# Row-tiled maxima in runs of two pairs, with K, V and Q in the output bank of V

## The chip, the cores and the metric

One core of a Trainium2 chip runs one program. The metric is its device time in microseconds. A time difference of less than half a per cent is not told from none here.

## What is computed

`x` is 2048 tokens by 128. The layer is a LayerNorm, attention with 16 heads of 64, and a mixture of 8 experts of which each token takes one, all added to `x`:

```python
xn = _layernorm(x)
q, k, v = (xn @ Wq), (xn @ Wk), (xn @ Wv)           # each cut into 16 heads of 64
attn = softmax(q @ k.T * 64 ** -0.5)                # per head, 2048 x 2048
attention = (attn @ v) @ Wo + bo
expert_ids = argmax(softmax(xn @ router_w.T))
h = square(relu(xn @ expert_fc[e]))                 # 128 -> 512
ffn = h @ expert_proj[e].T                          # 512 -> 128, of each token's own expert
return x + attention + ffn
```

## The kernel before, in words

Heads go in pairs (8 pairs), and a pair's queries in 4 chunks of 512: 32 blocks, written out one after another. Block n handles two heads and 512 queries. The instructions of each engine are one hand-written order; engines meet at semaphores.

A block has 16 steps `kt`, one for each tile of 128 keys. In a step, TensorE (PE) computes the scores of both heads, transposed: keys on partitions, queries along 512 columns. Each score is two matmuls into one of three banks `SB` (`high_scores`, `low_scores`), since Q and K are split into a high and a low part of fp32r: `K1` holds K's high part twice, `Q1` Q's high part in the 64 rows of the head's own half and the low part in the other half; `K2` and `Q2` carry K's low part, a row of ones and a row of minus the maximum. So the maximum is already subtracted when the bank is full. ACT takes the exponential of each bank (`exps`) into `EX`. After step 15 PE multiplies V by the exponentials (`times_v`), both heads in 64 columns each side by side in the bank `OB`, fp32, and ACT copies `OB` to `osb` (`take_o`). POOL adds the exponentials of one head, and of the other up to step 8 or 9; DVE adds the rest behind the scores. `fold_sums` (a transpose and a reduce of 512 columns) and `sum_parts` (five small steps) make the reciprocal row; SyncE stores it and spreads it to 128 partitions, POOL scales (`normalise`), and PE multiplies by Wo (`project`).

The maxima that block n+1 needs are made in block n, one matmul of [128 x 128] x [128 x 512] for each of 32 units (2 heads, 4 query tiles, 4 key chunks), one behind each score tile, into a ring of three banks `MB` (`max_unit`); DVE reduces each bank to one column (`maxima`). Block 0's own maxima are made ahead of it from 64 rows of each head, two heads as a pair (`max_pair`), with one reduce of 1024 columns for both (`maxima_pair`).

The eighth bank `XB` takes what comes in between: Q of block n+2 (step 14), V of the pair (steps 1, 2, 6, 8 of its first block), K of the next pair (steps 2 and 7 of its second and third block), the experts' products (steps 4 and 11), and Wo. `take_spare` makes each user of the bank wait until the one before has been read.

ACT copies a K or Q product into `high`, DVE makes `low` from the product minus `high`, and SyncE issues six DMAs that put the two into `K1`, `K2` or `Q1`, `Q2`. `high` may be written again only when those have landed: this is `staging_free`, a wait of ACT. For Q in a block that also makes K, it waits for both K chunks of that block. `K1` and `K2` have one semaphore for each parity of the pair (`d_k`).

SyncE's queue is in one order for each block, `one(n)` in its part: first K chunk (`spread_k`), row store and spread (`store_row`, `spread_rd`), the tokens of the next tile (`load_tokens`, four DMAs), second K chunk, Wo's weights, the expert's result (`store_tile`), the expert's weights (`load_tile`: a register is read from `owner_i`, then two DMAs), the maxima row (`place_max`), Q (`spread_q`). The tokens are sorted by expert into 23 tiles of 128; a tile goes with each of the blocks 5 to 27. POOL's indirect DMAs sort the tokens in blocks 1 to 3 (`SORT`) and fetch the results in blocks 28 to 30.

In the blocks of `LATE` the sums of the second head are folded in step 1 of the next block, in the others behind the scores.

## Time and profile before

| | |
|---|---|
| median of 3 runs | 1355.83 us (1352.04 to 1357.24) |
| profiled execution | 1357.17 us, its span 1355.4 us |
| PE busy | 1333.3 us, 98% |
| DVE busy | 1199.6 us, 89% |
| POOL busy | 1121.8 us, 83% |
| ACT busy | 708.4 us, 52% |
| mean granted clock of TensorE | 0.988 |

The span is from the first instruction to the last on the core. A matmul's record is longer than its distance to the next, since matmuls are pipelined: what one costs is seen from one start to the next. A block of the middle takes 39.6 us, 41.0 us when it makes K, and 43.2 us when it makes V. The clock is at half for the first 53 us but for one short stretch, and then at full.

### The profile page before, as it was taken

Reading aid. Unit: us, or ns where it says so; the run is one execution under the profiler, and the core shown is the slowest. Engines: PE = TensorE matmul, PEld = TensorE weight load, DVE = VectorE, ACT = ScalarE, POOL = GpSimd, SP = SyncE. Lnnn points to the kernel's source line nnn. Section 1 sums busy time; section 2 is a strip of 40 time slices with the busy share of each in tenths; the row PEclk is TensorE's granted clock in tenths of the full one; section 3 lists DMA queues with packets and bytes.
Section 4 is the critical chain, followed back from the end, with each engine's and each line's share of the span. In section 5 each row is a group of like instructions: output and inputs, shape, how many; then the busy total and the mean of one; then the engine's idle time right before and its main releaser. Section 6 shows DMA issues by size and latency. Waiting matters only on the chain.

```text
span 1355.4 us, 20239 instructions
## 1 busy us (share of the span) xinstructions
PE 1333.3 (98%) x6268; PEld 865.0 (64%) x6268; DVE 1199.6 (89%) x1890; ACT 708.4 (52%) x1230; POOL 1121.8 (83%) x884
## 2 busy tenths in 40 slices
PE   6999999999999999999999999999999999999998
PEld 3656667666676666776666766666766667765554
DVE  7788998998988899889988899889898899989997
ACT  4454556444565444664445664445654446654453
POOL 6779989787987778977788877879878789888997
PEclk8799999999999999999999999999999999999999
DMA  4223311233203222124212241124311143011101
GB/s 117 77 55 83 100 31 41 68 85 75 52 28 86 71 71 51 51 64 100 50 43 57 72 103 34 42 57 100 75 47 38 41 101 94 14 37 34 41 17 40
DMA packets 85867, 82.76 MB, mean 61 GB/s; under 512 B 24512, under 2 KB 54912, under 8 KB 85760
## 3 DMA queue, kind: packets, MB, share of 16 engines
q1 hardware_dynamic: 84736, 79.38, 23.5%
q0 software_dynamic: 1024, 2.10, 0.5%
q8 instruction: 50, 0.82, 0.3%
q14 instruction: 57, 0.47, 0.1%
HBM read 27.00 MB, written 6.29 MB: 25 GB/s over the span
## 4 chain that ended last, share of the span: by engine, by line
PE 93%; DVE 4%; ACT 1%; issue 1%; DMA 0%; POOL 0%; DVEq 0%; POOLq 0%
PE OB L1182 33%; PE SB L1127 16%; PE SB L1134 16%; PE MB L1153 15%; PE XB L1220 3%; PE XB L1210 2%; PE XB L1115 2%; PE XB L1108 2%; DVE low L935 2%; ACT high L677 1%; DVE mx L785 1%; PE XB L1191 1%; PE XB L1189 1%; PE XB L1190 1%; PE OB L1090 1%
## 5 line engine op out<-in xcount | busy, mean ns | idle before, releaser
L539 POOL TENSOR_TENSOR acc<-acc,ex 128x512 f32<-128x512 f32 x691 | 912.1, 1345 | 29.5 <-ACT ex L663 1.6
L785 DVE TENSOR_REDUCE mx<-MB 128x1 f32<-128x512 f32 x992 | 652.0, 684 | 72.5 <-PE MB L1153 71.5
L663 ACT ACTIVATE ex<-SB 128x512 f32<-128x512 f32 x1024 | 608.5, 599 | 103.9 <-PE SB L1134 40.2
L1182 PE MATMUL OB<-ex,V 128*64 128x512 f32 x2048 | 447.2, 594 | 0.0
L1127 PE MATMUL SB<-Q,K 128*128 128x512 f32 x1024 | 411.6, 402 | 0.0
L1134 PE MATMUL SB<-Q,K 128*128 128x512 f32 x1024 | 400.2, 391 | 0.0
L1153 PE MATMUL MB<-K,Q 128*128 128x512 f32 x992 | 389.5, 393 | 1.5 <-DVE mx L785 1.5
L1182 PEld LDWEIGHTS OB<-ex,V 128*64 128x64 f32 x2048 | 143.9, 137 | 277.8 <-issue 274.2
L821 DVE TENSOR_TENSOR acc<-acc,ex 128x512 f32<-128x512 f32 x205 | 285.2, 1391 | 20.1 <-DVE acc L821 0.9
L693 ACT ACTIVATE osb<-OB 128x512 f32<-128x512 f32 x32 | 19.2, 599 | 458.4 <-PE OB L1182 458.4
L1127 PEld LDWEIGHTS SB<-Q,K 128*128 128x128 f32 x1024 | 192.9, 188 | 66.4 <-issue 27.6
L539 POOL TENSOR_TENSOR acc<-ex 128x512 f32<-128x512 f32 x63 | 79.9, 1290 | 177.3 <-ACT ex L663 169.5
L1153 PEld LDWEIGHTS MB<-K,Q 128*128 128x128 f32 x992 | 186.4, 188 | 51.4 <-DVE mx L785 11.3
L1134 PEld LDWEIGHTS SB<-Q,K 128*128 128x128 f32 x1024 | 193.1, 189 | 35.7
L950 DVE STREAM_TRANSPOSE rd<-acc 128x512 f32<-128x512 f32 x62 | 44.0, 710 | 4.7 <-POOL acc L539 1.1
L952 DVE TENSOR_REDUCE halves<-rd 128x16 f32<-128x512 f32 x62 | 42.5, 686 | 2.2
L544 POOL TENSOR_TENSOR osb<-osb,rd 128x512 f32<-128x512 f32 x31 | 40.4, 1304 | 2.6 <-DMA rd<-rows_rd 2.6
L1220 PEld LDWEIGHTS XB<-wo,osb 128*128 128x128 f32 x248 | 30.2, 191 | 14.0 <-DVE low L935 13.8
L935 DVE SCALAR_TENSOR_TENSOR low<-XB,high 128x512 fp32r<-128x512 f32 x31 | 21.4, 692 | 18.6 <-ACT high L677 18.6
L1220 PE MATMUL XB<-wo,osb 128*128 128x128 f32 x248 | 35.7, 287 | 1.6
L1210 PEld LDWEIGHTS XB<-wraw,xT 128*128 128x128 f32 x256 | 33.9, 193 | 2.7 <-ACT V L687 0.2
L1210 PE MATMUL XB<-wraw,xT 128*128 128x128 f32 x256 | 34.0, 276 | 0.0
(135 smaller groups left out, 630.0 us busy)
## 6 DMA issues: line engine op xcount, KB each, us to landing
Q<-high SPq DMA_DIRECT2D x124, 128.0 KB, 2.3
K<-high SPq DMA_DIRECT2D x112, 128.0 KB, 2.3
Q<-low SPq DMA_DIRECT2D x64, 128.0 KB, 2.3
rd<-rows_rd SPq DMA_DIRECT2D x62, 128.0 KB, 2.9
K<-low SPq DMA_DIRECT2D x56, 128.0 KB, 2.4
w<-fc SPq DMA_DIRECT2D x23, 256.0 KB, 2.8
w<-projT SPq DMA_DIRECT2D x23, 256.0 KB, 3.1
sorted_x<-res SPq DMA_DIRECT2D x1, 1472.0 KB, 6.8
```

The costliest lines, as they stand in the source:

```text
L539: pool.tensor_tensor(a[:, :], src[:, :], EX[h][kt][:, :], ALU.add).then_inc(done, 1)
L663: act.activation(EX[h][kt][:, :], SB[bank_of(n, 2 * kt + h)][:, :], ACT.Exp).then_inc(a_e[h], 1)
L785: dve.tensor_reduce(mx[:, m % 2, u:u + 1], MB[bank_of(m, i)][:, :], AX.X, ALU.max).then_inc(v_m, 1)
L821: dve.tensor_tensor(a[:, :], src[:, :], EX[0][kt][:, :], ALU.add).then_inc(sums[0][n % 2], 1)
L935: dve.scalar_tensor_tensor(out=low[:, :], in0=XB[:, :], scalar=SCALE, in1=high[:, :], op0=ALU.mult, op1=ALU.subtract).then_inc(v_q, 1)
L950: dve.transpose(turned[:, :], acc[h][n % 2][:, :]).then_inc(v_turn, 1)
L1127: pe.matmul(SB[bank_of(n, 2 * kt + h)][:, :], K1[par][h][:, keys], Q1[k][h][:, :], start=True, stop=False)
L1134: pe.matmul(SB[bank_of(n, 2 * kt + h)][:, :], K2[par][h][:, keys], Q2[k][h][:, :], start=False, stop=True).then_inc(t_s, 1)
L1153: pe.matmul(MB[bank_of(m, i)][:, :], Q1[k][h][:, q * P:(q + 1) * P], K1[par][h][:, c * QB:(c + 1) * QB], start=True, stop=True).then_inc(t ...
L1182: mm = pe.matmul(OB[own[h], :], V[:, k, own[h]], EX[h][k][:, :], start=(k == 0), stop=(k == NT - 1))
L1210: mm = pe.matmul(XB[:, k * P:(k + 1) * P], xT[:, tok], wraw[pair % 2][:, 2, :], start=True, stop=True)
L1220: mm = pe.matmul(XB[:, q * P:(q + 1) * P], on[:, q * P:(q + 1) * P], wo_s[pair % 2][:, :], start=True, stop=True)
```

## The change

All blocks now get their maxima from the 64 rows of each head's own half, that is from the high parts alone, two heads as a pair. The pairs come in runs of two, at the even steps (in block 0 at steps 4, 5, 7, 8, 10, 11, 13, 14), in four banks `MB`. `XB` is gone: it is the fourth bank of `MB`. K, V and Q products go through `OB`, V's output bank, K at steps 1 and 5, V at 1, 3, 5, 7, Q at 11. The first V moves in front of block 0, between its pairs. Wo and the experts' two products move to the end of the block, ahead of V's product, into the banks of `MB`; the first product of a tile is made one block ahead of the second. Four small steps of the sums (`sum_parts`) move behind the scores where the block is not in `LATE`; in `LATE`, now without block 3, they stand at steps 3, 5, 7, 9. In the queue of SyncE, the expert's weights are loaded ahead of the second K chunk, with a register read for each, and the result is stored last. The experts and the sorting start one block earlier.

```diff
@@ constants
-AT_Q, AT_WO, AT_ON = 14, 13, 6
-AT_V, AT_K, AT_LOW = (1, 2, 6, 8), (2, 7), 5
-AT_UP, AT_DOWN = 4, 11
+AT_Q, AT_WO = 11, 13
+AT_V, AT_K, AT_LOW = (1, 3, 5, 7), (1, 5), 9
 TILES = NT + E - 1
-TILE0 = 5
+TILE0 = 4
...
-LATE = (0, 1, 2, 3, NB - 4, NB - 3)
+LATE = (0, 1, 2, NB - 4, NB - 3)
@@ banks
-        MB_all, SB_all = bank("MB", 3), bank("SB", 3)
+        MB_all, SB_all = bank("MB", 4), bank("SB", 3)
...
-        OB, XB = bank("OB"), bank("XB")
+        OB, FB = bank("OB"), MB[3]
+        WO_B, DOWN_B, UP_B, WO_LAST, SUM_B = MB[0], MB[1], MB[2], MB[2], MB[3]
@@ where maxima stand
-        def units(n, kt, h):
...
+        def runs(n, kt):
+            places = (4, 5, 7, 8, 10, 11, 13, 14) if n.off == 0 else range(0, NT, 2)
+            if n.off == NB - 1 or kt not in places:
                 return []
...
+            i = places.index(kt)
+            return [2 * i, 2 * i + 1]
@@ kv_job
-            if j == 0 and kt in AT_V:
+            if j == 0 and n.off and kt in AT_V:
@@ ahead of block 0
-        BETWEEN = {0: ("t", 2), 2: ("t", 3), 5: ("k", 2), 6: ("q", 1), 7: ("r", 0), 8: ("k", 3), 9: ("r", 1), 10: ("r", 2),
-                   11: ("r", 3)}
+        BETWEEN = {0: ("t", 2), 2: ("t", 3), 4: ("k", 2), 5: ("v", 0), 6: ("k", 3), 7: ("q", 1), 8: ("r", 0), 9: ("v", 1),
+                   10: ("r", 1), 11: ("v", 2), 12: ("r", 2), 13: ("v", 3), 14: ("r", 3)}
@@ SyncE
-                def load_tile(r):
...
-                    e = sp.value_load(owner_i[0:1, bass.ds(r.place(1), 1)], min_val=0, max_val=E - 1)
...
+                def expert(r):
+                    return bass.ds(sp.value_load(owner_i[0:1, bass.ds(r.place(1), 1)], min_val=0, max_val=E - 1), 1)
+
+                def load_up(r):
+                    wait(sp, t_up, r.times(1))
+                    sp.dma_start(w1[:, :], fc[expert(r), :, :].rearrange("e d h -> d (e h)")).then_inc(d_up, 16)
+
+                def load_down(r):
+                    wait(sp, t_down, r.times(1))
+                    sp.dma_start(w2[:, :, :], projT[expert(r), :, :].rearrange("e (c p) d -> p (e c) d", p=P)).then_inc(d_down, 16)
...
-                    if has_tile(n + 1):
-                        load_tokens(n + 1 - TILE0)
+                    for r in tile_up(n + 1):
+                        load_tokens(r)
+                    for r in tile_up(n):
+                        load_up(r)
+                    for r in tile_down(n):
+                        load_down(r)
                     for job in kv_job(n, AT_K[1]):
                         if job[0] == "k":
                             spread_k(*job[1:])
...
-                    if has_tile(n):
-                        store_tile(n - TILE0)
-                    if n.off == TILE0 - 1:
-                        sp.wait_ge(v_own, 1)
-                    if has_tile(n + 1):
-                        load_tile(n + 1 - TILE0)
                     if n.off < NB - 1:
                         place_max(n + 1)
                     if n.off < NB - 2:
                         spread_q(n + 2)
+                    for r in tile_down(n):
+                        store_tile(r)
@@ POOL
-                        if kt == AT_ON and not (n.i is None and n.off == 0):
+                        if n.off and kt == (8 if n.off - 1 in LATE else 6):
                             normalise(n - 1)
@@ DVE
                     for kt in range(NT):
-                        for h in range(2):
-                            for m, u in units(n, kt, h):
-                                maxima(m, u)
+                        for p in runs(n, kt):
+                            maxima_pair(n + 1, p)
                         if 0 < n.off < NB - 1:
-                            late = n.off - 1 in LATE
-                            if late and kt == 1:
-                                fold_sums(n - 1, 1)
-                            sum_parts(n - 1, kt - late)
+                            if n.off - 1 in LATE:
+                                if kt == 1:
+                                    fold_sums(n - 1, 1)
+                                if kt % 2:
+                                    sum_parts(n - 1, kt // 2)
...
                         if n.off not in LATE:
                             fold_sums(n, 1)
-                        if n.off == NB - 2:
                             for part in range(1, 5):
                                 sum_parts(n, part)
@@ PE
-                def max_unit(m, i, u=None):
...
+                def max_pair(m, p):
...
+                        if p < 2:
+                            boundary_read(m - 2)
+                        wait(pe, v_m, m.times(UNITS, 2 * p - 2))
...
+                    for h in range(2):
+                        pe.matmul(PAIR[m.off > 0][p % 2][:, h * QB:(h + 1) * QB], Q1[k][h][own[h], q * P:(q + 1) * P],
+                                  K1[par][h][own[h], c * QB:(c + 1) * QB], start=True, stop=True).then_inc(t_m, 1)
...
                 def project(n):
-                    take_spare(v_y, n.times(1, 1))
+                    into = WO_B if n.off < NB - 2 else WO_LAST
+                    if n.off < NB - 2:
+                        wait(pe, v_m, (n + 3).times(UNITS, -2))
...
                             low_scores(n, kt, h)
-                            for m, u in units(n, kt, h):
-                                max_unit(m, u)
-                        if has_tile(n):
-                            if kt == AT_UP:
-                                expert_up(n - TILE0)
-                            if kt == AT_DOWN:
-                                expert_down(n - TILE0)
+                        for p in runs(n, kt):
+                            max_pair(n + 1, p)
...
                             project(n - 1)
+                        for r in tile_down(n):
+                            expert_down(r, n)
+                        for r in tile_up(n):
+                            expert_up(r, n)
                         times_v(n, 0, NT)
```

## Rows read from the trace of the kernel before

In a row of a timeline: start in us, duration in us, engine, line, operation, output<-inputs, count, and in brackets the idle time in front of it with what ended it. In a row of windows: the stretch, its length, busy time and count of PE, PEld, DVE, ACT and POOL, the granted share of TensorE's clock, the DMA share, GB/s.

**Rows 1.** The page, part 1: busy time and share of the span.

```profile
PE 1333.3 (98%) x6268; PEld 865.0 (64%) x6268; DVE 1199.6 (89%) x1890; ACT 708.4 (52%) x1230; POOL 1121.8 (83%) x884
```

**Rows 2.** The page, part 4: the chain that ended last.

```profile
PE 93%; DVE 4%; ACT 1%; issue 1%; DMA 0%; POOL 0%; DVEq 0%; POOLq 0%
```

**Rows 3.** Busy time by engine in block 5, V product to V product.

```profile
279.73:320.71 40.98, 40.92 (x195) 26.89 (x194) 37.52 (x59) 21.99 (x38) 34.23 (x27) 1.00 0.39 97
```

**Rows 4.** The page, part 5: exponentials and V products.

```profile
L663 ACT ACTIVATE ex<-SB 128x512 f32<-128x512 f32 x1024 | 608.5, 599 | 103.9 <-PE SB L1134 40.2
...
L1210 PE MATMUL XB<-wraw,xT 128*128 128x128 f32 x256 | 34.0, 276 | 0.0
```

**Rows 5.** Timeline of PE, full clock, into and out of the 64-column V product.

```profile
76.45 0.39 PE L1134 MATMUL SB<-Q,K 128*128 128x512 f32 x1
...
77.35 0.39 PE L1153 MATMUL MB<-K,Q 128*128 128x512 f32 x1
77.67 13.95 PE L1182 MATMUL OB<-ex,V 128*64 128x512 f32 x64
...
91.56 0.50 PE L1127 MATMUL SB<-Q,K 128*128 128x512 f32 x1
91.89 0.40 PE L1134 MATMUL SB<-Q,K 128*128 128x512 f32 x1
```

**Rows 6.** Timeline of PE, half clock, around the 64-row pairs of block 0.

```profile
15.14 0.63 PE L1190 MATMUL SB<-xhi,wlo 128*128 128x512 f32 x1
15.57 0.63 PE L1191 MATMUL SB<-xlo,whi 128*128 128x512 f32 x1
...
40.80 0.79 PE L1167 MATMUL MB<-K,Q 64*128 64x512 f32 x2
41.40 0.63 PE L1167 MATMUL SB<-K,Q 64*128 64x512 f32 x2
...
44.15 0.80 PE L1167 MATMUL SB<-K,Q 64*128 64x512 f32 x2 [0.34 <-DVE mx L791]
44.87 1.65 PE L1153 MATMUL MB<-K,Q 128*128 128x512 f32 x3
```

**Rows 7.** Timeline of DVE, two reduces of pairs back to back.

```profile
42.88 1.22 DVE L791 TENSOR_REDUCE mx<-SB 128x2 f32<-128x1024 f32 x1
44.01 1.22 DVE L791 TENSOR_REDUCE mx<-MB 128x2 f32<-128x1024 f32 x1
```

**Rows 8.** Timeline of the SyncE queue in block 6.

```profile
300.06 1.11 SPq L356 DMA_DIRECT2D K<-high  x2
...
303.14 0.60 SPq L356 DMA_DIRECT2D K<-low  x1
303.85 0.53 SPq L407 DMA_DIRECT2D rows_rd<-halves  x1
...
308.90 1.13 SPq L356 DMA_DIRECT2D K<-high  x2
...
311.99 0.60 SPq L356 DMA_DIRECT2D K<-low  x1
313.75 0.34 SPq L444 DMA_DIRECT2D sorted_y<-res  x1
315.08 0.37 SPq L438 DMA_DIRECT2D w<-fc  x1
```

**Rows 9.** Timeline of ACT in block 6: the copies into high.

```profile
298.71 0.60 ACT L683 ACTIVATE high<-XB 128x512 fp32r<-128x512 f32 x1 [0.31 <-PE XB L1191]
...
318.24 0.60 ACT L677 ACTIVATE high<-XB 128x512 fp32r<-128x512 f32 x1 [0.31 <-PE XB L1191]
```

**Rows 10.** The page, part 6: issue to landing.

```profile
K<-low SPq DMA_DIRECT2D x56, 128.0 KB, 2.4
```

**Rows 11.** Timeline of PE at the end of block 6: last maximum, Wo.

```profile
319.18 0.39 PE L1153 MATMUL MB<-K,Q 128*128 128x512 f32 x1
319.62 1.16 PE L1220 MATMUL XB<-wo,osb 128*128 128x128 f32 x8
```

More of the change, by code:

```diff
@@ L676, in high_q @@
                         staging_free(act, "q", m)
-                    act.activation(high[:, :], XB[:, :], ACT.Copy, scale=SCALE).then_inc(a_q, 1)
+                    act.activation(high[:, :], (FB if m.off == 1 else OB)[:, :], ACT.Copy, scale=SCALE).then_inc(a_q, 1)
                 def kv(kind, pair, c):
@@ new lines, in max_pair, with boundary_read @@
+                    for h in range(2):
+                        pe.matmul(PAIR[m.off > 0][p % 2][:, h * QB:(h + 1) * QB], Q1[k][h][own[h], q * P:(q + 1) * P],
+                                  K1[par][h][own[h], c * QB:(c + 1) * QB], start=True, stop=True).then_inc(t_m, 1)
+                def boundary_read(n):
+                    if n.off < 0:
+                        pe.wait_ge(v_mask, 2)
+                    else:
+                        wait(pe, v_y, n.times(1))
+                        for r in tile_up(n):
+                            wait(pe, a_up, r.times(1, 1))
+                        for r in tile_down(n):
+                            wait(pe, a_res, r.times(1, 1))
@@ L1219, in project @@
                     for q in range(TB):
-                        mm = pe.matmul(XB[:, q * P:(q + 1) * P], on[:, q * P:(q + 1) * P], wo_s[pair % 2][:, :],
+                        mm = pe.matmul(into[:, q * P:(q + 1) * P], on[:, q * P:(q + 1) * P], wo_s[pair % 2][:, :],
                                        start=True, stop=True)
@@ L1257, in first @@
                             logits(c)
-                    for u in range(MIDDLE):
-                        max_unit(Lin(1), u)
                     pe.wait_ge(v_m, UNITS)
```

191 lines of the change are left out of this document (83 added, 108 removed).

## The prediction

> **What bounds the kernel now.** I read the page first, then the chain, then one block after another. TensorE (PE) is busy for 98% of a span of 1355.4 us, DVE for 89% [rows 1], and 93% of the chain that ended last is PE [rows 2]. In block 5, PE works for 40.92 of 40.98 us at full clock, DVE for 37.52, POOL for 34.23, ACT for 21.99 [rows 3]. So PE's own instructions make the period, and no other engine is waited for. The block has two halves. Behind the scores stand 13.9 us of V product in which DVE and POOL finish the sums. In front of it stand 27 us of scores and maxima, and here ACT must turn 32 score tiles at 0.599 us each [rows 4] and DVE must reduce everything that PE leaves. A saving on PE in that half is worth something only as far as ACT, DVE, and what these two wait for keep up.
>
> I make the sum against the profiled execution, 1357.17 us with a span of 1355.4; the median of the runs is 1355.83, so 1.3 us come off at the end.
>
> **The maxima on PE.** At full clock a 512-column matmul follows the last after 0.225 to 0.23 us (four steps from 76.45 to 77.35) [rows 5]; I use 0.2275. A block spends 32 x 0.2275 = 7.28 us on maxima. Afterwards it has eight runs of two pairs, at even steps. Do the two heads of a pair really run side by side? In block 0 they do: a pair of 64-row matmuls takes 0.79 us at half clock and 0.63 behind another one, like one single matmul (0.63) [rows 6]. So a run holds two slots, 0.455 us, and the four changes around it. Their price at full clock is in no row for 64 rows; I bound it. The nearest at full clock is the 64-column V product: 0.32 from the last 128-wide matmul into it, so 0.09 extra, and the second gap after leaving it is 0.33, so 0.10 extra [rows 5]. At half clock, where the ordinary gap is 0.43, pair to pair takes 0.60, pair to single 0.72, and the next two gaps together 1.02 of three matmuls' 1.65 [rows 6]: 0.17 + 0.29 + 0.16 extra, half of it if it goes by the clock. I take 0.09 in, 0.08 between, 0.09 out, 0.10 behind: 0.36. A run costs 0.815 us, eight 6.52. The gain is 0.76 us in each of blocks 1 to 30: -22.8. Below it could be nothing (0.455 a run, gain 3.6 a block), above 0.77 (1.225 a run, loss 2.5).
>
> A rule bears on this. The rows say that a change of shape costs about 0.1 us per gap on PE [rows 5]. The Trainium skill (TensorEngine Tiling (Array Packing), Tiling Modes, Key Properties) says that changing the mode drains the engine, and that is what speaks against many short runs. By that rule the saving of 3.6 us a block would be mostly spent, as the rows also have it.
>
> **Wo.** The last maximum stands 0.44 us ahead of Wo's product instead of 0.2275, since XB waits for DVE's Q subtraction [rows 11]. Now Q is made at step 11 in V's bank, and Wo in MB waits only for the reduce of the second last pair; that ends some 1.8 us after the last run began, and the run and step 15 take PE 1.7, so I leave nothing of the stall. 30 x 0.216 = -6.5.
>
> **The ring of maxima.** A reduce of a pair takes 1.22 us and follows the last after 1.13 [rows 7]. Two steps take 8 x 0.2275 + 0.815 = 2.635 us on PE; DVE needs 2.27 of them, so 0.37 is over. It can't be used as slack for long: the second pair of a run waits for the reduce of the second pair of the run before, which ends about 0.5 + 1.13 + 1.22 us after that run began, and stands 0.3 into its own run. That is a floor of about 2.6 us for two steps, hardly under PE's 2.635. What DVE does between two runs beyond 0.37 us, PE waits for, unless PE has an extra product there too. Q's product (0.68 us, step 11) has; I put its subtraction at nothing. In blocks 3, 29 and 30 the fold of the late head's sums stands at step 1: a transpose and a reduce of 512 columns, which I take as a little over one pair's reduce, 1.4 us. 3 x 1.0 = +3.1. In the six V blocks 4 to 24 the weights' subtraction stands at step 9; for it I take one reduce, 1.13 - 0.37 = 0.75: +4.5. ACT with 2 x 2 x 0.6 = 2.4 in 2.635 keeps up.
>
> Moving four DVE steps of the sums (1.5 us) from between the maxima to the end of a block costs nothing: they lie under the V product. DVE's tail grows from 14.8 to some 16.4 us, and it now begins about 1.4 us before the V product; 13.9 + 1.4 + 1.6 us until the next first pair is ready is 16.9. Without that cover it would be 1.5 a block.
>
> **The copies into high, and the SyncE queue.** This is the term that decides. K, V and Q products are all copied by ACT, and for K and Q into one buffer, `high`, which may be overwritten only when six DMAs of the last K chunk, issued by SyncE one by one, have landed. Take block 6, where the scores begin at 293.61. The first K copy is at 298.71, its DMAs are issued from 300.06 to 303.74; then the queue does the row store, waits for its landing, spreads the row, loads tokens, and only at 308.90 comes to the second chunk, whose last issue is at 311.99 [rows 8, 9]. It lands 2.4 us later [rows 10], at 314.4. Q's copy comes at 318.24 [rows 9]. So 3.8 us are spare.
>
> All of that is used up. K now comes at steps 1 and 5, Q at step 11 instead of 14. Block start plus 1.02 us is the first run; steps 2 to 10 follow at 2.635 per two, K products at 0.68. So the first copy stands at 3.6 us from the block's start, the second at 9.6, Q's at 18.2 (24.6 before). Meanwhile the queue: first chunk issued from 4.95 to 8.6; row, landing and tokens 5.16 as before, to 13.8; and then, in front of the second chunk and no longer behind it, both expert weight loads. Each now reads the owner itself: 0.99 from the end of the store at 314.09 to the load at 315.08, and 0.37 to 0.40 for the issue [rows 8]: 2.75. The second chunk is issued from 16.55 to 20.2 and lands at 22.0. ACT stands at Q's copy from 18.2 to 22.0 with every exponential of steps 12 to 15 queued behind it, and DVE stands at Q's subtraction with the reduces of the last four pairs behind it. PE can fill three banks of scores and one run, then waits: exponential 24 ends near 23.2, the reduces of the run at step 12 run from 23.3 to 25.65, so the run at step 14 ends at 26.05 and the scores at 27.0, against 23.25 without the wait. That is 3.8 us. (The second K copy also waits, for the landing of the first chunk at 10.5, up to 0.9 us; it is inside this number, because 22.0 is fixed by the queue.) Twelve blocks have K and experts: +45.6.
>
> Blocks 1 and 2 have K and no experts, but their row is ready only after step 9 of DVE, about 16.3 us from the start. Store and spread take 5.16 - 2.1, the second chunk lands at about 24.8, 2.8 later than above: 6.6 each, +13.2.
>
> **Prologue and block 0.** Block 0's four V products (34.0 / 32 = 1.06 us each [rows 4]) move in front of it, between pairs where the clock is half: about 1.75 each there. Some of it falls into gaps in which PE waited for DVE (0.34 at 44.15 [rows 6]). Three maxima leave the prologue. But in block 0 the eight runs stand between steps 4 and 14, two of them adjacent, which is DVE's pace. I take +3, between 0 and +6.
>
> **Sum.** 1357.2 - 22.8 - 6.5 + 3.1 + 4.5 + 45.6 + 13.2 + 3 = 1397.3; less 1.3, 1396.
>
> **Rivals.**
> (a) The landing is in time and PE's saving stays. For it: the queue is idle for long stretches, and the 3.8 us at Q are a difference of two times of about 20 each. It needs the second chunk to land 3.8 us sooner than I have it; that is the point from which it decides, and each microsecond on the way is worth 12 to 14. Then the terms of 45.6 and 13.2 fall, some 6 stay for the second K copy: 1344, faster.
> (b) Changes of shape cost what they cost at half clock, 0.77 a run. 3.3 us more in each of some 17 blocks without K, and about 0.8 in the 14 others (there the later Q eats the wait): 1396 + 56 + 11 = 1463. Against it: the V product's gaps at full clock.
> (c) PE falls to half clock. PE then sits idle 3 us on end in 14 blocks; all of block 5 was at full clock [rows 3], and it never idled so. Half clock doubles a gap (0.43 for 0.2275 [rows 5, 6]). If a stretch as long as the wait is lost so, 3.3 us cost 1.7 more: +24, 1420.
> (d) The change does little: the wait is half as long (-29) and the changes of shape cost half. The latter gives 1.4 us in each of six V blocks, where V's product keeps the run clear of DVE, and elsewhere only down to the ring's floor, 0.3 in each of 16 blocks without a landing to wait for: -13. 1396 - 29 - 13 = 1354, no difference.
> The Trainium skill (TensorE: Matmul & The Clock Gate, Part 3: Packing small matmuls) puts matmuls on different rows some 4 ns apart; the pairs here show one time for both [rows 6], and it changes none of this.
>
> **How the numbers follow.** Main case 0.48, with its own range 1378 to 1415. (a) 0.19, (b) 0.08, (c) 0.12, (d) 0.13. Likeliest: 1396. The range takes in the upper part of (a) and reaches to between (c) and (b): 1340 to 1435, with about 0.1 left out on either side. A difference under 0.5% (6.8 us) is about what runs of this kernel can't tell from none. Faster 0.20 ((a) and a little of (d)), same 0.12, slower 0.68.
>
> **What would show it.** Right: in blocks 5, 6, 9, 10 and so on ACT's Q copy is released by a K DMA and not by PE, 3 to 4 us late; PE has gaps there ended by DVE or ACT; the K blocks are 43 to 44 us long and the block behind each second K block (7, 11, ...) about 0.9 shorter than 39.6. The two weight loads stand ahead of the second K chunk in the queue. PE's busy share falls below 95%. Runs of pairs: 0.3 us between pairs, the next score 0.3 later. Wrong: if Q's copy follows its matmul by 0.03 us in K blocks, the queue was quicker, and (a) holds; if the gaps around pairs are 0.5 and more, (b).

## The result, and the profile after

The changed kernel takes 1489.97 us (median of four runs, 1486.45 to 1496.98) against 1356.26 for the kernel before, a ratio of 1.0996, 95% interval 1.0954 to 1.1038. Forecast were 1396 and a range to 1435: the direction was right, the size was not. The profiled execution took 1492.15 us, its span is 1490.3, so 134.9 more than the 1355.4 of before.

The page of the changed kernel, parts 1 and 4, and groups of part 5 (busy and mean of one, then the engine's idle time before them and what ended it):

```profile
PE 1370.8 (92%) x6268; PEld 748.0 (50%) x6268; DVE 1153.8 (77%) x1393; ACT 645.6 (43%) x1230; POOL 1106.6 (74%) x885
...
PE 71%; SPq 10%; issue 6%; DVE 6%; DMA 5%; ACT 1%; ACTq 0%; POOL 0%; DVEq 0%; POOLq 0%
...
L1154 PE MATMUL MB<-K,Q 64*128 64x512 f32 x1008 | 208.8, 480 | 59.1 <-DVE mx L790 59.0
...
L830 DVE TENSOR_TENSOR wlo<-wraw,whi 128x256 fp32r<-128x256 f32 x8 | 58.5, 7311 | 0.0
...
L681 ACT ACTIVATE high<-OB 128x512 fp32r<-128x512 f32 x30 | 17.9, 598 | 52.1 <-DMA K<-low 48.8
```

PE was 98% of its span and 93% of the chain [rows 1, 2]; now it is 92% and 71%. Two waits are new. ACT stands 48.8 us at Q's copy for the DMAs of K: the forecast's term. And PE stands 59.0 us at the maxima for DVE's reduces, which nobody had forecast. The line that explains it has only eight instructions: the weights' subtraction (`low_w`, L830) takes 7.3 us in the mean. In the kernel before the same eight take between 0.39 and 1.37 us:

```profile
L831 DVE TENSOR_TENSOR wlo<-wraw,whi x8: 393/1356/1370, 8.4 to 1045.6; 128x256 fp32r<-128x256 f32 x8
```

Where in the program the time went, by windows of the changed kernel: about a K block (scores of block 6), one with neither K nor V (7), and a V block (8); the columns are those of [rows 3].

```profile
324.80:370.80 46.00, 42.73 (x195) 23.25 (x193) 33.81 (x42) 19.95 (x38) 33.05 (x26) 0.96 0.29 72
370.80:410.70 39.90, 39.90 (x190) 21.49 (x188) 33.60 (x34) 18.71 (x36) 33.87 (x26) 1.00 0.17 44
410.70:450.60 39.90, 32.12 (x159) 22.17 (x159) 32.20 (x32) 21.13 (x41) 32.17 (x26) 0.87 0.08 22
```

The first two stretches run from a block's first score to the next block's; the third has the scores of block 8 alone and ends where its V product begins (the whole block takes 53.7 us, 43.2 in before). The plain block (39.90 us, 39.6 in before) is full. In the K block PE is idle for 3.3 us and the clock is 0.96, in the V block it is idle for 7.8 us and the clock is 0.87.

**The V block.** Timelines of DVE, POOL and PE of the changed kernel in block 8:

```profile
428.07 1.22 DVE L790 TENSOR_REDUCE mx<-MB 128x2 f32<-128x1024 f32 x1
429.20 9.60 DVE L830 TENSOR_TENSOR wlo<-wraw,whi 128x256 fp32r<-128x256 f32 x1
438.72 2.34 DVE L790 TENSOR_REDUCE mx<-MB 128x2 f32<-128x1024 f32 x2
...
413.96 2.52 POOL L542 TENSOR_TENSOR acc<-ex 128x512 f32<-128x512 f32 x2 [5.20 <-ACT ex L667]
416.44 1.04 POOL L551 TENSOR_TENSOR up<-up 128x512 f32<-128x512 f32 x1
417.43 9.99 POOL L542 TENSOR_TENSOR acc<-acc,ex 128x512 f32<-128x512 f32 x8
427.35 1.32 POOL L547 TENSOR_TENSOR osb<-osb,rd 128x512 f32<-128x512 f32 x1
428.60 12.72 POOL L542 TENSOR_TENSOR acc<-acc,ex 128x512 f32<-128x512 f32 x10
...
439.99 0.80 PE L1154 MATMUL MB<-K,Q 64*128 64x512 f32 x2 [7.39 <-DVE mx L790]
441.12 0.79 PE L1154 MATMUL MB<-K,Q 64*128 64x512 f32 x2 [0.34 <-DVE mx L790]
442.43 0.63 PE L1131 MATMUL SB<-Q,K 128*128 128x512 f32 x1
442.86 0.63 PE L1124 MATMUL SB<-Q,K 128*128 128x512 f32 x1
```

DVE has nothing to wait for at 429.20 (no idle time in front of it), and this subtraction takes 0.35 us when POOL rests (`a_low_late` below). Here it ends only at 438.8. POOL meanwhile makes one addition in SBUF after the other; the first gap between two of them, 0.143 us, begins at 438.51, when for once two additions to the same head follow each other. So the subtraction lasted over eight additions in a row, and it ended 0.28 us after the last of them. In all 32 subtractions of the layer that were held up like this, in whatever kernel, the end comes 0.28 to 0.29 us after the addition in front of POOL's first gap. PE has its banks full and waits 7.39 us, and behind this idle time its clock is at half: scores follow at 0.43 instead of 0.23 us until 445.4. 7.4 + 0.3 + half of the last 5.4 is 10.4 us, and the V block is 10.4 longer. The six V blocks 4 to 24 are 9.9 to 10.7 longer.

**The K block.** Timelines of SyncE's queue, ACT and PE in block 6, which begins at 324.8, for the rows of [rows 8, 9]:

```profile
332.93 0.60 SPq L355 DMA_DIRECT2D K<-low  x1
...
336.59 2.01 SPq L419 DMA_DIRECT2D tok<-sorted_x  x4
339.58 0.37 SPq L438 DMA_DIRECT2D w<-fc  x1
340.74 0.42 SPq L442 DMA_DIRECT2D w<-projT  x1
341.20 1.15 SPq L355 DMA_DIRECT2D K<-high  x2
...
344.32 0.60 SPq L355 DMA_DIRECT2D K<-low  x1
...
335.32 0.60 ACT L687 ACTIVATE high<-OB 128x512 fp32r<-128x512 f32 x1 [0.70 <-DMA K<-low]
348.20 0.60 ACT L681 ACTIVATE high<-OB 128x512 fp32r<-128x512 f32 x1 [4.19 <-DMA K<-low]
...
349.34 0.50 PE L1124 MATMUL SB<-Q,K 128*128 128x512 f32 x1 [3.03 <-ACT ex L667]
```

As forecast: tokens, two weight loads with a register read each, then the second K chunk, issued from 16.4 to 20.1 us after the block's start (forecast 16.55 to 20.2). Q's copy, which its landing releases, starts at 23.4 (forecast 22.0; 21.6 to 23.7 over the twelve K blocks), and PE waits 3.03.

Block by block, from the start of one V product to the next in the two traces, summed by kind; the forecast's column adds up its own terms:

| us more than before | forecast | changed | `a_low_late` | `a_loads_back` | `a_three` | `a_three_k7` |
|---|---|---|---|---|---|---|
| ahead of the first V product | +3 | 0.0 | -3.0 | -2.1 | +6.5 | +1.9 |
| blocks 1, 2 | +11.2 | +16.1 | +16.6 | +16.7 | +4.0 | +1.8 |
| 12 with K and experts | +33.9 | +50.8 | +52.0 | +13.5 | +9.5 | -0.9 |
| 6 with V (4 to 24) | -1.4 | +62.0 | +0.9 | +62.5 | -0.5 | -0.7 |
| 6 plain (7 to 27) | -5.9 | +0.7 | +0.7 | +0.8 | -0.5 | -0.5 |
| 3, 28, 29, 30 | -0.8 | +4.4 | +3.9 | +4.8 | +4.0 | +4.9 |

The experts' tiles begin one block earlier now: block 4 has one of their products that it did not have, block 27 has one less. So the plain blocks 7 to 23, which have the same work as before, are 0.24 to 0.28 us longer each in the changed kernel, and block 27 is 0.65 shorter.

### The profile page after: what moved, and what is told of

The parts are those of the page before. It is cut to its first block, busy times and chain, and to the rows that moved or that the text cites. A ratio compares the mean times of both kernels' runs of the same rounds, so it can differ in the third digit from the quotient of the medians.

```text
span 1490.3 us, 20436 instructions
## 1 busy us (share of the span) xinstructions
PE 1370.8 (92%) x6268; PEld 748.0 (50%) x6268; DVE 1153.8 (77%) x1393; ACT 645.6 (43%) x1230; POOL 1106.6 (74%) x885
## 4 chain that ended last, share of the span: by engine, by line
PE 71%; SPq 10%; issue 6%; DVE 6%; DMA 5%; ACT 1%; ACTq 0%; POOL 0%; DVEq 0%; POOLq 0%
PE OB L1181 30%; PE SB L1124 13%; PE SB L1131 10%; PE MB L1154 8%; SPq L355 6%; DVE mx L790 4%; DMA K<-low 3%; PE MB L1219 2%; DMA rows_rd<-halves 2%; PE OB L1207 2%; PE MB L1112 1%; SPq L419 1%; PE MB L1104 1%; SPq L411 1%; SPq L434 1%
## 5 line engine op out<-in xcount | busy, mean ns | idle before, releaser
L790 DVE TENSOR_REDUCE mx<-MB 128x2 f32<-128x1024 f32 x504 | 591.8, 1218 | 193.6 <-PE MB L1154 190.7
L667 ACT ACTIVATE ex<-SB 128x512 f32<-128x512 f32 x1024 | 542.5, 602 | 260.5 <-PE SB L1131 258.8
L1124 PE MATMUL SB<-Q,K 128*128 128x512 f32 x1024 | 454.1, 444 | 39.9 <-ACT ex L667 38.5
L1131 PE MATMUL SB<-Q,K 128*128 128x512 f32 x1024 | 415.2, 406 | 0.0
L820 DVE TENSOR_TENSOR acc<-acc,ex 128x512 f32<-128x512 f32 x204 | 251.1, 1231 | 28.2 <-ACT ex L667 5.7
L1154 PE MATMUL MB<-K,Q 64*128 64x512 f32 x1008 | 208.8, 480 | 59.1 <-DVE mx L790 59.0
L1154 PEld LDWEIGHTS MB<-K,Q 64*128 64x128 f32 x1008 | 87.5, 192 | 175.9 <-DVE mx L790 105.5
L934 DVE SCALAR_TENSOR_TENSOR low<-OB,high 128x512 fp32r<-128x512 f32 x30 | 20.6, 688 | 53.4 <-ACT high L681 53.4
L830 DVE TENSOR_TENSOR wlo<-wraw,whi 128x256 fp32r<-128x256 f32 x8 | 58.5, 7311 | 0.0
L681 ACT ACTIVATE high<-OB 128x512 fp32r<-128x512 f32 x30 | 17.9, 598 | 52.1 <-DMA K<-low 48.8
L1219 PE MATMUL MB<-wo,osb 128*128 128x128 f32 x248 | 35.7, 289 | 4.2 <-issue 2.2
L1219 PEld LDWEIGHTS MB<-wo,osb 128*128 128x128 f32 x248 | 32.4, 198 | 12.6 <-DVE mx L790 8.6
```

The lines of the kernel that those rows point to most:

```text
L667: act.activation(EX[h][kt][:, :], SB[bank_of(n, 2 * kt + h)][:, :], ACT.Exp).then_inc(a_e[h], 1)
L790: dve.tensor_reduce(mx[:, m % 2, u:u + TB * JB + 1:TB * JB], PAIR[m.off > 0][p % 2].rearrange("p (a k) -> p a k", a=2), AX.X, ALU.max).the ...
L820: dve.tensor_tensor(a[:, :], src[:, :], EX[0][kt][:, :], ALU.add).then_inc(sums[0][n % 2], 1)
L830: dve.tensor_tensor(wlo[k][:, :, :], wraw[k][:, 0:2, :], whi[k][:, :, :], ALU.subtract).then_inc(v_w, 1)
L1124: pe.matmul(SB[bank_of(n, 2 * kt + h)][:, :], K1[par][h][:, keys], Q1[k][h][:, :], start=True, stop=False)
L1131: pe.matmul(SB[bank_of(n, 2 * kt + h)][:, :], K2[par][h][:, keys], Q2[k][h][:, :], start=False, stop=True).then_inc(t_s, 1)
```

## The experiments

Two theories for the V blocks. **Lock-out:** POOL's gapless additions keep DVE off SBUF, and whatever moves the subtraction away from them or opens a gap gives the 10 us back. **Rival:** the V block is slow for another reason that shows as a long subtraction (V's products in `OB`, the late Q, the clock). Where one time is given, it is that of a single run; the kernel before took 1354.9 to 1357.0 us beside it.

**The subtraction moved.** In the changed kernel to the end of the block, where POOL rests:

```diff
-                        if kt == AT_LOW and n % JB == 0 and n.off < NB - JB:
-                            low_w(n // JB + 1)
...
                             fold_sums(n, 1)
...
+                        if n % JB == 0 and n.off < NB - JB:
+                            low_w(n // JB + 1)
```

> The changed kernel, with one edit: DVE's subtraction of the split weights (wlo) stands behind the folds of the sums at the end of a V block instead of at step 9. In the changed kernel it lasts 9.6 us in the six V blocks 4 to 24 (8.6 in block 4), and PE stands 7.4 us behind it. Theory A (it has two inputs in SBUF and can't start while POOL's adds follow each other without a gap): under the V product POOL's adds have gaps or are over, it lasts under 2 us and PE waits for none of it, V blocks go from 53.6 to 42-44 us, the whole from 1490 to 1415-1430. Rival B (what is slow is the operation itself or its data, ACT's high part): it lasts 9 us at the new place too, and what it delays is the next block's maxima; total within 15 us of 1490.

1428.02 us. The subtraction takes 0.35 us in the six V blocks (0.93 in block 0), they lose 0.9 instead of 62.0 (table), and the other kinds of block keep theirs. So the 61 us hang on this one instruction and its place.

```profile
L830 DVE TENSOR_TENSOR wlo<-wraw,whi x8: 348/349/928, 8.4 to 1138.8; 128x256 fp32r<-128x256 f32 x8
```

And in the kernel before to step 9, the other way round (`AT_LOW = 9` for 5):

> The kernel before, with one number changed: the subtraction of the split weights at step 9 instead of 5. Theory A (locked out by POOL's run of adds, which at steps 6 to 9 has no gap): it lasts 6 to 10 us instead of 1.3 in the V blocks, the maxima behind it are late, PE waits 5 to 8 us in each of seven V blocks and falls to half clock there: 1356 goes to 1400-1430. Rival C (the lock-out needs the new order of the maxima or the new banks): it stays 1.3 us, and the time 1356 within 5.

1396.35 us, 41 slower, a little under what was expected:

```profile
L831 DVE TENSOR_TENSOR wlo<-wraw,whi x8: 391/5081/8659, 8.4 to 1082.6; 128x256 fp32r<-128x256 f32 x8
```

Four of its V blocks have a subtraction of 8.66 us, two not (1.30 and 1.50). The rival is out: no other part of the change is in this kernel. But why not all six?

**What opens it.** POOL takes the heads in turn about, so that every second addition is to the head of the one before and waits for it (a gap of 0.143 us):

```diff
-                        if on_pool(n, kt):
-                            add(n, kt, 0)
-                        add(n, kt, 1)
+                        for h in (0, 1) if kt % 2 else (1, 0):
+                            if h or on_pool(n, kt):
+                                add(n, kt, h)
```

> The changed kernel, with one edit: POOL takes the two heads in turn about (first head first in odd steps, second head first in even ones), so that every second add waits for the add right before it and a gap of about 0.14 us opens between them, as now only from step 10 on. The subtraction on DVE stays at step 9. Theory A: it gets in at the first such gap, after at most two or three adds, so it lasts 1 to 3.5 us instead of 9.6; V blocks lose 6 to 9 us, total 1430-1450. Rival B (its own slowness) and rival D (it waits for the end of the first head's adds on POOL as such): 8 to 10 us as now, total 1485-1500.

1434.58 us, subtractions of 1.35 to 1.55 in all V blocks. It fits, but five of the six were let in between two additions without a gap, so the gap at that place can't be the whole rule.

The subtraction at step 5 in the changed kernel (`AT_LOW = 5`), in one run and then in four:

> The changed kernel, with one number set back: the subtraction of the split weights at step 5, as in the kernel before. Theory A in its strict form (it always has to wait for the first gap between POOL's adds): POOL is at its third step then and has no gap up to step 10, so it lasts 15 to 18 us, V blocks grow by 6 to 8 us more, total 1525-1545. Theory A in its loose form (a boundary between two adds without a gap can let it in, as it did in the kernel before at this step, and doesn't always): it lasts 1.3 us in some or all V blocks, total 1425 if in all.

> The changed kernel with the weights' subtraction at step 5, once more, in rounds. If step 5 is a place where DVE is always let in (as in all eight V blocks of the kernel before), all runs stand within 3 us of 1434. If it is drawn anew in each execution, the runs scatter over 1434 to 1495.

1434.15 us, then 1432.2 (1428.56 to 1437.57; ratio 1.0562, 1.0524 to 1.06). 0.74 to 1.0 us in each V block, in both traces.

**A result that misled.** Maxima from all 128 rows, the rest of the change as it is:

```diff
-                        pe.matmul(PAIR[m.off > 0][p % 2][:, h * QB:(h + 1) * QB], Q1[k][h][own[h], q * P:(q + 1) * P],
-                                  K1[par][h][own[h], c * QB:(c + 1) * QB], start=True, stop=True).then_inc(t_m, 1)
+                        rows = slice(0, P) if m.off else own[h]
+                        pe.matmul(PAIR[m.off > 0][p % 2][:, h * QB:(h + 1) * QB], Q1[k][h][rows, q * P:(q + 1) * P],
+                                  K1[par][h][rows, c * QB:(c + 1) * QB], start=True, stop=True).then_inc(t_m, 1)
```

> The changed kernel, with one edit: behind block 0 each maximum is made from all 128 rows again (high and low part of Q), at the same steps, in the same banks and order, so the maxima are slightly other numbers and PE never changes its shape for them. My reading of the trace: a run of two 64-row pairs takes 0.865 us with its changes, four 128-row matmuls 0.91, so a block that waits for nothing else (7, 11, 15, ...) goes from 26.07 to 26.4, and the total moves by 0 to +10. Rival (the changes of shape cost more than they give): the block falls below 25.8 and the total by 10 or more. Rival (64 rows free of cost for the change, 0.5 us a run): the block goes to 28.5 or more.

> The changed kernel with maxima from 128 rows, once more, in rounds. One locked V block costs about 10 us, so the times alone tell how many of the six are locked in each execution: none 1435, all six about 1497. If 128-row maxima keep DVE from being locked out, all runs stand within 3 us of 1435. If the lock-out is drawn anew in each execution, the runs scatter over 1435 to 1495, in steps of about 10.

The first run gave 1434.84, 55 less than the change, with no subtraction over 1.24: as if the pairs were to blame. Four more gave 1491.08 (1486.2 to 1495.46), in the traced one all subtractions of blocks 4 to 24 at 8.6 to 9.6. The same program has both outcomes, in different executions and on different chips; which of the two it hangs on isn't told apart. One time alone is no verdict here; only the trace says which outcome it was. In the one without lock-outs a plain block (7 to 23) takes 26.16 us from its first score to its V product, against 25.99 with 64 rows: the pairs side by side, the heart of the change, are worth 0.17 us a block.

Q at step 14 instead of 11 (`AT_Q = 14`), in one run and then in six:

> The changed kernel, with one number set back: Q's product at step 14 instead of 11. Theory (Q's copy waits for the landing of the second K chunk, fixed by the queue at 22 to 23.7 us from the block's start): the copy's own turn now comes at about 22.7, so it waits for 0 to 1 us, the 12 blocks with K and experts lose 3 to 5 us each, blocks 1 and 2 about 4; total 1425-1445. V blocks stay at 53.6. Rival (what costs is the number of DMAs or ACT's order, not the place of Q): total above 1470.

> The kernel with Q at step 14 once more, timed. In its first run the subtraction was locked out in blocks 0, 8, 12 and 24 and not in 4, 16 and 20. If the lock-out is a matter of the program's fixed timing, the same blocks show it again and the times agree within 0.5% of 1416. If it is drawn anew in each execution, other blocks show it and the times scatter by steps of about 11 us (a few between 1380 and 1450).

1416.48 us with three of six V blocks locked (8, 12 and 24, and block 0 too, with 7.17 us); then six runs from 1422.98 to 1448.32, with six of six locked in the profiled one (1439.09). Against the changed kernel, also with six of six, that is 51 us less: the late Q gives back its share. Which V blocks are locked differs between the two executions.

**The loads behind the second K chunk**, as they were in before, in the changed kernel:

```diff
+                    for job in kv_job(n, AT_K[1]):
+                        if job[0] == "k":
+                            spread_k(*job[1:])
                     for r in tile_up(n):
                         load_up(r)
                     for r in tile_down(n):
                         load_down(r)
-                    for job in kv_job(n, AT_K[1]):
-                        if job[0] == "k":
-                            spread_k(*job[1:])
```

> The changed kernel, with one edit: in SyncE's queue the two loads of the experts' weights stand behind the second K chunk again. Theory (the prediction's): the second chunk is issued 2.5 us earlier in the twelve blocks with K and experts, Q's copy on ACT then starts about 2.5 us earlier (near 20 instead of 22.0 to 23.7 us from the block's start), and each such block is 2.5 to 4 us shorter, more where it now loses the full clock: 1490 goes to 1445-1460. Blocks 1 and 2, which have no experts, and the V blocks stay. Rival: Q's copy is held by the row store's landing, not by the loads; then the blocks lose less than 1 us each and the total stays above 1480.

1453.96 us. Q's copy comes 19.3 to 21.1 us after the block's start instead of 21.6 to 23.7, and the twelve K blocks lose 13.5 instead of 50.8. The loads in front of the K chunk, 2.75 us by the forecast, cost 3.1 in each block. Of that 2.0 are idle time of PE (32.0 us more than before over the twelve, with the loads back 7.6). The rest fits the clock: seven of the twelve have 27.3 us at half clock together, half of which is 13.7 us or 1.1 a block, and with the loads back none has any.

**The three repairs together** (subtraction late, loads back, Q at 14), and with the second K product at step 7 for 5 besides:

> The changed kernel with three edits together: the subtraction behind the sums, the experts' weights behind the second K chunk, Q at step 14. If these two waits are all that the change costs beyond its own small terms, 62 + 55 to 65 us go and 1365-1375 remain; the rest then stands in blocks 1, 2, 29 and 30 (DVE's folds between the maxima) and is not in blocks 3 to 28, which are then level with the kernel before within 0.5 us. Rival (the ring of two pairs or the changes of shape cost by themselves): blocks 3 to 28 stay 1 us or more longer than before, total 1385 or more. Rival (the prediction's saving of 1 us a block is real and was only covered): total 1345-1360.

> The kernel of the three edits, and K's second chunk at step 7 instead of 5. In it the second K copy waits up to 1 us, more where a DMA lands late, for the landing of the first chunk (copies at 10.5 to 13.1 us from the block's start). Theory: with step 7 its turn comes at about 12.3, it waits for nothing in most K blocks, these lose 0.3 to 1.5 us each; total 1382 to 1370-1376. Rival: Q's copy then waits for the later second chunk; K blocks stay or grow, total 1380 or more.

1381.77 and 1364.32 us. The first is 7 us above what was expected: the twelve K blocks still lose 9.5, and the stretch ahead of the first V product is 6.5 longer. In the table's last column every kind of block is back at before's time or a little under it, but for blocks 1, 2, 29 and 30. So the losses are accounted for, and what is left of the gain is on average under 0.15 us a block: 0.3 in the V blocks 8 to 24, nothing in the plain ones (7 to 23: 0.04 to 0.10 longer than before).

**What decides the lock-out.** Three small kernels of their own: POOL adds in SBUF in rounds, DVE asks for the subtraction at shifted moments. The core of the first (`alt` makes two chains in turn about, which leave no gap):

```python
for k in range(14):                                  # POOL
    h = k % 2 if alt else 1
    wait(pool, done[h], i - 1)
    pool.tensor_tensor(acc[h][:, :], acc[h][:, :], ex[h][:, :], ALU.add).then_inc(done[h], 1)
...
dve.wait_ge(done[h], i)                              # DVE, after the second addition
dve.tensor_reduce(mx[:, :], big[:, 0:c], AX.X, ALU.max).then_inc(v_mx, 1)     # c shifts it
dve.tensor_tensor(wlo[:, :], raw[:, :], whi[:, :], ALU.subtract).then_inc(v_sub, 1)
```

> A kernel of its own for the disputed wait; it leaves out the whole layer (its output is sums of x). Forty rounds: POOL makes 14 adds of 128x512 in SBUF, DVE a maximum over PSUM of 64 to 1216 columns (to shift it) and then the subtraction of 128x256 from SBUF to SBUF. In half of the rounds POOL alternates between two sums (each add starts before the last ends), in the other half it adds to one sum (a gap of 0.14 us between adds). No PE, no ACT. Theory A strict (locked out until a gap): alternating rounds show 8 to 16 us whatever the shift, the others 0.4 to 1.7. Theory A loose (a boundary without a gap lets it in by luck of timing): alternating rounds show both 0.4-1.7 and many microseconds, depending on the shift, repeatably for the same shift. Rival (it needs PE's or ACT's traffic as well): all rounds under 2 us.

None of 40 locked (0.42 to 1.50 us: the rest of the addition under way, and 0.28), gapless or not; 18 of the 20 gapless ones came after 16 to 130 additions in a row. The lock-out needs more than DVE and POOL. With ACT and PE working beside them:

> A small kernel of its own (it computes nothing of the reference): POOL does rounds of 14 adds of 512 columns in SBUF, DVE one subtraction of 256 columns in SBUF at a start that shifts from round to round. Forty rounds with ACT taking exponentials from PSUM into SBUF beside them, forty with PE multiplying, forty with both, all with two chains of adds that follow without a gap, then twenty of both with one chain. If the lock-out needs the traffic of another engine, several subtractions of the forty in that kind of round take 5 us and more, and none of the single chain over 1.5. If it needs neither, but something else of the kernel (the DMAs, the place in the program), all stay at 0.4 to 1.5 us as in the first small kernel.

The lock-out is there: of 120 gapless rounds 52 have subtractions of 13.3 to 14.7 us; with one chain (a gap of 0.143 after each addition) none of 20. Sorted by what went before, a pattern stands out. Where only two or three additions had passed since POOL's last gap, none of 52 was locked; where 16 to 59 had, 52 of 68 were. Of these 68, ACT alone worked in 20 rounds, and all 20 were locked, though ACT's last exponential had ended 4.4 to 5.6 us before DVE asked; with PE alone it was 15 of 25, with both 17 of 23. So either engine is enough, and ACT need not be at work when DVE asks. In the layer's traces, over subtractions that came while POOL was at work, the pattern is the same: up to seven POOL instructions since the last gap, none of 46; nine, none of 8; ten, one of 5; twelve or thirteen, 31 of 42. (Block 8 above: 2 + 1 + 8 + 1 = 12 finished since the gap of 5.20. The kernel before with step 9: block 4 asks one instruction after a gap, the five others after thirteen, of which block 12 was let in.) So this number alone was varied, POOL at rest before each round:

> A third small kernel (it computes nothing of the reference), ACT and PE working beside throughout. Every round starts with POOL idle; then two chains of adds follow without a gap, and DVE asks for its subtraction after 1, 3, 5, 7, 9, 11, 13, 17 or 21 of them, each at eight shifts; nine more adds follow. If DVE is kept out only once POOL has gone on without a gap for long, none of the rounds with up to 7 adds ahead is locked and a good part of those with 11 and more is. If the number of adds doesn't matter, the locked ones (some two in five, as in the rounds with both engines before) are spread over all nine.

| additions ahead since POOL's last gap | 1 | 3 | 5 | 7 | 9 | 11 | 13 | 17 | 21 |
|---|---|---|---|---|---|---|---|---|---|
| locked, of 8 | 0 | 0 | 0 | 0 | 1 | 5 | 2 | 8 | 8 |

A long row makes the lock-out likely here and not certain: in the kernel before this one, 16 of the 68 were let in with 16 to 45 additions ahead.

Two of its rounds with the same shift, 13 and 17 ahead; timelines of DVE and of POOL:

```profile
623.46 0.84 DVE L115 TENSOR_TENSOR wlo<-raw,whi 128x256 fp32r<-128x256 f32 x1
658.50 11.83 DVE L115 TENSOR_TENSOR wlo<-raw,whi 128x256 fp32r<-128x256 f32 x1
...
606.57 28.66 POOL L74 TENSOR_TENSOR acc<-acc,ex 128x512 f32<-128x512 f32 x23 [1.39 <-DVE mx L119]
636.62 33.43 POOL L74 TENSOR_TENSOR acc<-acc,ex 128x512 f32<-128x512 f32 x27 [1.39 <-DVE mx L119]
```

The first subtraction is let in behind the addition under way. The second is shut out until POOL's row ends (658.50 + 11.83 = 670.3; 636.62 + 33.43 = 670.1).

In the changed kernel, POOL's order swapped at one step of the V blocks alone, early, which shortens the gapless row in front of the subtraction from 12 to 5 and leaves the place of the subtraction gapless:

```diff
-                        if on_pool(n, kt):
-                            add(n, kt, 0)
-                        add(n, kt, 1)
+                        for h in (1, 0) if kt == 3 and n.off % 4 == 0 and n.off else (0, 1):
+                            if h or on_pool(n, kt):
+                                add(n, kt, h)
```

> The changed kernel; only in the six V blocks, POOL takes the two heads in the other order at step 3, so two adds of one head follow each other there, twice, and leave 0.14 us each; then some 6 to 8 adds without a gap precede the weights' subtraction where there were 12. If the length of the gapless row decides, all six subtractions take under 1.6 us in every execution and the time is 1430 to 1438. If the lock-out is chance whatever went before, most are locked: 1470 to 1495.

> The changed kernel with the weights' subtraction at step 7, between step 5 (six adds ahead, never locked) and step 9 (twelve, mostly locked): about nine ahead. If the length of the gapless row decides and eight are enough, the times stand at 1470 to 1495; if twelve are needed, 1430 to 1438; in between if nine is on the border.

1432.77 us (1429.84 to 1448.95; ratio 1.0597, 1.0524 to 1.0671), subtractions of 0.42 and 1.37 to 1.39. Two gaps of 0.143 us, the later one 6 us ahead of the subtraction, are worth 57 us. With the subtraction at step 7 (`AT_LOW = 7`), nine ahead: 1437.78 (1435.02 to 1439.94), 0.87 to 1.11 in all six of the traced run; nine were few enough there, where one of eight was locked with nine ahead in the small kernel.

**A version that beats both.** The kernel before with Q at step 12 for 14, which moves Q's subtraction out of the way of Wo:

> The kernel before, with one number changed: Q's product at step 12 instead of 14. It tests the term of the prediction for Wo's wait (0.216 us in each of 30 blocks, since XB is still being read by DVE's subtraction): the gap of 0.44 between the last maximum and Wo's product goes to 0.23, the blocks of the middle lose 0.2 us each, total 1356 to 1349-1351. Q's copy at about 21.7 us from the block's start is still behind the landing of the second K chunk (20.8), so no new wait. Rival: the wait moves to the score behind it or to a late landing; total 1354 or more.

1347.46 us (1342.7 to 1348.06; ratio 0.9943, 0.9922 to 0.9964), half a per cent. Wo now follows the last maximum after 0.22 us, for 0.44 in [rows 11]:

```profile
317.43 0.39 PE L1153 MATMUL MB<-K,Q 128*128 128x512 f32 x1
317.65 1.05 PE L1220 MATMUL XB<-wo,osb 128*128 128x128 f32 x8
```

## Why the prediction was wrong

**The step that failed** is "in the six V blocks 4 to 24 the weights' subtraction stands at step 9; for it I take one reduce, 1.13 - 0.37 = 0.75: +4.5". The six blocks lost 62.0 us; with the subtraction elsewhere 0.9. Of the 94 us between forecast and result it makes 63 (from -1.4 to +62.0). The price was taken from DVE's work; it is POOL that sets it. There was a sign in the trace of before: the subtraction took 1.36 us in the median and 0.39 at the least, and in each V block it ended 0.28 us after one of POOL's instructions, so it already waited a microsecond for POOL. The bound on the other side was there too: the rest of POOL's row of additions, eight of 1.24, 9.9 us. Neither row was read, and the range had no such end.

The Trainium skill (SBUF — State Buffer, SBUF: two separate sides) says that GpSimd and a DVE operation with two inputs in SBUF hold a shared port as an exclusive lock for a whole instruction. The traces agree for one instruction: a subtraction that is let in takes 1.62 us at most, the rest of one addition included. They go beyond it in the rows of eight and more additions that DVE doesn't get between. That the shared port is what holds DVE off fits these rows; no run tests the port itself.

**The copies into high, +45.6:** the mechanism and its place were right, and the queue's times to 0.15 us up to the last issue. The landing came up to 1.7 us later than forecast. That the twelve blocks lost 50.8 where 33.9 was the sum of all their terms has two causes. PE's idle time grew by 32.0 us, not by 45.6; rival (c), priced beside the main case and not in it, put 27.3 us at half clock on top, in seven of the twelve blocks, and half of that is 13.7. Together 45.7: that the term's size came out is luck. The difference of 16.9 is mostly the saving on maxima and Wo that did not come: 1.24 a block, as in the plain blocks, is 14.9. Moving the loads back gave 37.3, Q, K and the loads together all 51.7. Blocks 1 and 2: +11.2 forecast, +16.1 measured, the same.

**The maxima, -22.8:** too high. A timeline of PE at full clock in block 7 of the changed kernel shows each term:

```profile
371.60 0.40 PE L1131 MATMUL SB<-Q,K 128*128 128x512 f32 x1
371.93 0.73 PE L1154 MATMUL MB<-K,Q 64*128 64x512 f32 x4
372.59 0.50 PE L1124 MATMUL SB<-Q,K 128*128 128x512 f32 x1
372.93 0.40 PE L1131 MATMUL SB<-Q,K 128*128 128x512 f32 x1
```

0.33 in, 0.66 for the two pairs and the way out, 0.34 behind, 1.33 together; two ordinary gaps of 0.23 less, a run is 0.87 (forecast 0.815). Every second run takes 0.95 (0.74 instead of 0.66 from its first pair to the next score), since its second pair waits for DVE's reduce: the ring's floor, which I had put just under PE's pace, is at times just over it. A run comes every 2.74 or 2.82 us in turn, for 2.635 forecast. And the scores between runs follow at 0.235 for 0.2275. Eight runs at 0.1 more and 48 gaps at 0.0075 more are 1.2 us: the plain blocks 7 to 23 lost 0.26 where -0.98 was forecast. Rival (b), 1.225 a run, did not come.

**Wo, -6.5:** right about the cause of the stall, as the kernel before with Q at 12 shows (0.32 us a block, 9.8 between the two spans): 0.22 is the gap, the other 0.1 is Wo's product itself, which takes 1.05 for 1.16. In the changed kernel little of it came: Wo starts 0.39 after the last score (393.55 to 393.94), because the reduce of its bank is 0.16 late, of which I had written 1.8 against 1.7.

**Smaller terms.** The folds: block 3 as forecast (0), blocks 29 and 30 +1.5 and +3.0 for about 0. The prologue: 0 for +3, but kernels that are alike there differ by -3.4 to +6.8 ahead of the first V product, so this says nothing.

**What stays open.** Why a long gapless row shuts DVE out, and what ACT or PE at work adds to it: the small kernels show that a short row never did it and that it never came without one of the two, not the mechanism. From nine additions on, their number alone doesn't tell a round that is locked from one that is not. Nor is it shown what part the chip has: the program with maxima from 128 rows had none locked on one chip and six of six on another, and the run with three of six was on the chip that had none. In the layer, additions overlap a little more in most locked stretches (0.05 to 0.09 us against 0.03 to 0.07), but not in all. One of the four runs of the kernel with one gap took 1448.95, 17 more than the others; it wasn't profiled, so a locked block in it isn't ruled out.

## What to carry to other kernels

Before a DVE operation with two inputs in SBUF is moved, look at what POOL does there: how many of its instructions have followed one another since its last gap, and how long the row still goes on. That rest of the row is what the move can cost at most. If the operation can't be moved, a gap of 0.14 us in POOL's order some instructions ahead of it was enough here. And where a forecast has PE idle for microseconds, the half clock behind it belongs in the main case.

## What the runs showed of the hardware

- A row of POOL additions in SBUF without a gap can keep a DVE subtraction out for its whole rest, 9.6 us in the layer and 14.7 in a small kernel. With up to seven instructions since POOL's last gap it never happened (46 cases in the layer, 32 in the small kernel); with nine to thirteen it came in some (32 of 55 and 8 of 24); with 16 and more in 68 of 84 (the two small kernels with ACT or PE at work). In the layer it ended at POOL's first gap each time (32 of 32; 0.14 us, once 0.17), in the small kernels at the end of the row.
- Without ACT and PE at work it didn't happen in 20 gapless rounds, after up to 130 additions. With ACT alone it came in 20 of 20 with 16 or 17 additions ahead, with PE alone in 15 of 25.
- The same program was locked in no V block in one execution (1434.84 us) and in all six in another, on another chip (1489.42).
- Two pairs of 64-row matmuls at full clock cost 0.87 us between scores of 128 rows, four slots for the price of 3.8, and the scores behind them follow at 0.235 instead of 0.2275.
